# A Mamba block and a quantised FFN on one core: the second weight part on VectorE, batch 0's block-diagonals through DRAM, and a new order

## The reference

```python
# cross attention in name: a selective scan over ctx_1024, gated by layernorm(x)
x  = einsum('bld,ed->bel', ctx, in_proj_w)            # 4 x 256 x 256
u  = silu(causal_conv4(x) + conv_b)
x_dbl = einsum('bdl,ed->bel', u, x_proj_w)
dt_low, B, C = split(x_dbl, [8, 16, 16])
dt = softplus(einsum('brl,dr->bdl', dt_low, dt_proj_w) + dt_proj_b)
for l in range(256):                                   # per channel d, state n
    h = h * exp(dt[l] * A) + dt[l] * u[l] * B[l]
    y[l] = sum_n h * C[l]
y  = (y + D * u) * silu(z)                             # z = layernorm(x_in)
x  = x_in + tanh(g_xattn) * y.T
# FFN on layernorm(x), inputs quantised to 8 bits per row, 256 -> 2*704 -> 256
x13 = quant(layernorm(x)) @ w13.T ; x1, x3 = split(x13)
g   = rmsnorm(relu(x1)**2 * x3) * norm_w
out = x + tanh(g_ffn) * (quant(g) @ w2.T)
```

## Time and profile before

| what | value |
|---|---|
| time of three runs | 192.03, 193.95, 194.18 us, median 193.95 |
| the profiled execution | 194.1 us, its span 192.3, mean granted clock 0.982 |
| busy: PE, DVE, ACT, POOL | 175.6, 165.0, 153.3, 123.2 us |
| DMA | 22.47 MB in 27314 packets |
| chain that ended last | PE 64%, DVE 11%, issue 9%, DMA 5%, POOL 4%, ACT 4% |

### The profile page before, as it was taken

How to read it: one execution, slowest core, us unless ns; L and a number is a source line. 1 busy time by engine, 2 the same in 40 slices (tenths; PEclk the granted TensorE clock), 3 DMA queues, 4 the chain that set the end, 5 groups by cost and what they waited for, 6 DMA issues and landing times.

```text
span 192.3 us, 3413 instructions
## 1 busy us (share of the span) xinstructions
PE 175.6 (91%) x1106; PEld 139.3 (72%) x1106; DVE 165.0 (86%) x267; ACT 153.3 (80%) x388; POOL 123.2 (64%) x88
## 2 busy tenths in 40 slices
PE   3978889998699999999999999999996999998994
PEld 1745867876689978966798786868764576786783
DVE  0699995999967999999999997998999989996462
ACT  3468996999929999999999998987994979375630
POOL 3020575993869799749999586999980997440000
PEclk9999978999799999999999999999999999999999
DMA  4794960058970634696530038851007100001011
GB/s 83 235 294 142 367 213 0 1 26 206 406 266 20 205 122 12 110 346 216 172 109 0 10 4 136 302 164 60 0 0 238 38 0 0 3 6 51 1 56 56
DMA packets 27314, 22.47 MB, mean 117 GB/s; under 512 B 15152, under 2 KB 21024, under 8 KB 27296
## 3 DMA queue, kind: packets, MB, share of 16 engines
q1 hardware_dynamic: 26752, 22.25, 40.3%
q10 hardware_dynamic: 544, 0.01, 0.2%
HBM read 18.98 MB, written 3.27 MB: 116 GB/s over the span
## 4 chain that ended last, share of the span: by engine, by line
PE 64%; DVE 11%; issue 9%; DMA 5%; POOL 4%; ACT 4%; SPq 3%; POOLq 0%; DVEq 0%
PE m_ps L1078 25%; PE y_ps L1102 12%; PE w_ps L1132 10%; PE w_ps L1149 4%; DMA ctx_in<-in_ctx 3%; POOL hb L409 3%; DMA cs<-c_rows 2%; PE w_ps L1043 2%; DVE hb L889 2%; PE y_ps L1090 1%; PE w_ps L1035 1%; DVE gt L956 1%; PE w_ps L1140 1%; DVE xc L814 1%; PE w_ps L1158 1%
## 5 line engine op out<-in xcount | busy, mean ns | idle before, releaser
L409 POOL TENSOR_TENSOR hb<-hb,cs 128x1024 f32<-128x1024 f32 x31 | 73.6, 2388 | 4.5 <-DVE hb L900 4.0
L900 DVE TENSOR_TENSOR_SCAN hb<-dA,m_ps 128x1024 f32<-128x1024 f32 x30 | 67.9, 2276 | 5.9 <-PE m_ps L1078 3.8
L1078 PE MATMUL m_ps<-bd,duT 128*128 128x256 f32 (+1 forms) x216 | 59.7, 420 | 1.5 <-ACT duT L703 0.8
L688 ACT ACTIVATE dA<-dt,nega 128x255 f32<-128x255 f32 (+1 forms) x144 | 54.9, 465 | 0.0
L1078 PEld LDWEIGHTS m_ps<-bd,duT 128*128 128x128 f32 x216 | 40.8, 199 | 12.0 <-issue 5.2
L1102 PE MATMUL y_ps<-identf,hb 128*128 128x128 f32 x256 | 33.2, 278 | 0.3 <-POOL hb L409 0.2
L1102 PEld LDWEIGHTS y_ps<-identf,hb 128*128 128x128 f32 x256 | 29.5, 143 | 4.4 <-issue 1.7
L1132 PE MATMUL w_ps<-w13T,xqT 128*128 128x352 bf16 x192 | 30.3, 313 | 0.1
L1132 PEld LDWEIGHTS w_ps<-w13T,xqT 128*128 128x128 bf16 x192 | 18.6, 98 | 9.6 <-ACT xqT L725 0.5
L1149 PE MATMUL w_ps<-w2T,iqT 128*128 128x256 bf16 x144 | 16.5, 273 | 0.0
L424 POOL TENSOR_TENSOR gw<-gg,normw 128x704 f32<-128x704 f32 x7 | 12.8, 1829 | 5.3 <-DVE gg L942 5.3
(11 more groups left out here) (143 smaller groups left out, 273.7 us busy)
## 6 DMA issues: line engine op xcount, KB each, us to landing
cs<-c_rows SPq DMA_DIRECT2D x16, 512.0 KB, 5.8
bd<-b_diag SPq DMA_DIRECT2D x10, 512.0 KB, 7.0
b_diag<-zeros SPq DMA_DIRECT2D x1, 2048.0 KB, 9.9
gw<-in_L_ffn_w SPq DMA_DIRECT2D x1, 1408.0 KB, 9.2
x<-in_x SPq DMA_DIRECT2D x1, 1024.0 KB, 5.4
out<-ctx_in SPq DMA_DIRECT2D x8, 128.0 KB, 1.7
ru<-in_L_ffn_w SPq DMA_DIRECT2D x1, 704.0 KB, 8.9
bd<-b_rows SPq DMA_DIRECT2D x2, 256.0 KB, 3.6
```

The lines of the kernel that those rows point to most:

```text
L409: E.tensor_tensor(h_g, h_g, cs[:, s0:s0 + sn, l0:l0 + ln], ALU.mult).then_inc(hc_end if (b, i, h) == OUT_END else hc_ok[h], 1)
L688: last = act_fn(dA_g[:, s, 1:ln], dt[:, p, h, l0 + 1:l0 + ln], ACT.Exp, scale=nega[:, h, s0 + s:s0 + s + 1])
L900: V.tensor_tensor_scan(hb[:, k % 3, h], dA[:, k % 2, h].rearrange("p n l -> p (n l)"), m_ps[:, h], 0.0, ALU.mult, ALU.add).then_inc(scan_o ...
L1078: last = T.matmul(m_q[:, :, c * P - l0:(c + 1) * P - l0], duT[:, p, c, h * P:(h + 1) * P], bd[:, (s0 + sn // 2 * q) // GN, c, n0:n0 + sn / ...
```

## The change

Two steps change engine or way, and all five lists of `PLAN` are written anew.

1. `w_mid` (nine copies of float32 to bfloat16) runs on VectorE.
2. Batch 0 gets its block-diagonals through the DRAM scratch like the others: `bT` on TensorE and `bd` on VectorE are gone; `bput/0.0` and `bget/0.0` to `bget/0.3` come to the sync queue, and `zero` and the first loads change places. For batch 0 `bget` waits for `bput` alone.

```diff
 def diagonals(b, g):
-    return sum(1 for a in range(1, b + 1) if a == BATCH - 1 or not by_pool(a, g))
+    return sum(1 for a in range(b + 1) if a == BATCH - 1 or not by_pool(a, g))
...
-        dt/0.1 bd/0.1 scan0/0.0 scan1/0.0 w_res/0.3 lowc/1.0 scan0/0.1 scan1/0.1 conv/2.0 scan0/0.2 series/1.0
+        dt/0.1 w_res/0.3 w_mid/0.1 lowc/1.0 w_mid/0.2 scan0/0.0 w_mid/0.3 scan1/0.0 scan0/0.1 scan1/0.1 conv/2.0
...
+        bget/2.0 bget/2.1 bget/2.2 bget/2.3 bput/3.0 cget/2.1 bget/3.0 mput/3.0 bget/3.1 cput/3.0 cget/2.2 cget/2.3
...
                 elif name == "bput":
                     sp.wait_ge(free["dve"], emptied("xdbl", b, 0))
-                    if b == 1:
+                    if b == 0:
                         sp.wait_ge(d_zero, 16)
...
                 elif name == "bget":
-                    sp.wait_ge(b_put, 16 * HALVES * b)
-                    taken(b, i)
+                    sp.wait_ge(b_put, 16 * HALVES * (b + 1))
+                    if b:
+                        taken(b, i)
...
-                elif name == "w_mid":
-                    n_, parts = wp_cols(i)
-                    act.wait_ge(free["dve"], emptied("w", 0, i))
-                    act_fn(parts[1], wres[:, i % 3, 0:n_], ACT.Copy).then_inc(wmid_ok, 1)
...
+                elif name == "w_mid":
+                    n_, parts = wp_cols(i)
+                    dve.wait_ge(free["dve"], emptied("w", 0, i))
+                    V.tensor_copy(parts[1], wres[:, i % 3, 0:n_]).then_inc(wmid_ok, 1)
...
-                        if b == 3:
-                            dve.wait_ge(b_put, 16 * HALVES)
+                        dve.wait_ge(b_put, 16 * HALVES * (b - 1))
...
-                            if b:
-                                g = (s0 + sn // 2 * q) // GN
-                                pe.wait_ge(b_got[g], 16 * diagonals(b, g))
-                            elif c < HALVES - 1:
-                                pe.wait_ge(bd_ok, i // 2 + 1)
-                            else:
-                                pe.wait_ge(free["dve"], emptied("bT", b, i // 2))
+                            g = (s0 + sn // 2 * q) // GN
+                            pe.wait_ge(b_got[g], 16 * diagonals(b, g))
```

More of the change, by code:

```diff
@@ L101 @@
+        down/2.1 iqT/3.1 down/3.0 down/3.1
     """,
     "act": """
[L103 to L106 removed]
@@ L132 @@
-        final/1.1 gate/3.2 gate/3.3 gated/3.1 absmax/3.1 scale2/3.1 quant2/3.1 final/2.0 final/2.1 outscale/3.1
-        final/3.0 final/3.1
+        winT/0.0 conv/0.0 conv/0.1 clamp/0.0 xstat/0.0 clamp/0.1 u/0.0 xstat/1.0 xstat/2.0 u/0.1 xstat/3.0 dtwT/0.0
+        lowc/0.0 gates/0.0 conv/1.0 series/0.0 clamp/1.0 dt/0.0 series/0.1 w_res/0.0 w_mid/0.0 w_res/0.1 w_res/0.2
+        dt/0.1 w_res/0.3 w_mid/0.1 lowc/1.0 w_mid/0.2 scan0/0.0 w_mid/0.3 scan1/0.0 scan0/0.1 scan1/0.1 conv/2.0
+        series/1.0 cubic/1.0 dt/1.0 scan0/0.2 w_res/0.4 w_res/0.5 du/1.0 scan1/0.2 clamp/2.0 scan0/0.3 w_mid/0.4
@@ new lines @@
+        scan1/0.3 w_mid/0.5 scan0/1.0 w_res/0.6 scan1/1.0 yz/0.0 w_res/0.7 x1/0.0 w_mid/0.6 scan0/1.1 absx1/0.0
+        w_mid/0.7 w_res/0.8 lowc/2.0 scan1/1.1 w_mid/0.8 scan0/1.2 conv/3.0 quant1/0.0 series/2.0 cubic/2.0 dt/2.0
+        scan1/1.2 gate/0.0 gate/0.1 du/2.0 scan0/1.3 scan1/1.3 gate/0.2 gate/0.3 clamp/3.0 absmax/0.0 scan0/2.0
+        yz/1.0 absmax/0.1 x1/1.0 scale2/0.0 lowc/3.0 scan1/2.0 scan0/2.1 absx1/1.0 outscale/0.0 quant1/1.0
+        series/3.0 scan1/2.1 quant2/0.0 scan0/2.2 gate/1.0 dt/3.0 gate/1.1 scan1/2.2 scan0/2.3 gate/1.2 gate/1.3
```

112 lines of the change are left out of this document (44 added, 68 removed).

## The result

| | kernel before | changed kernel |
|---|---|---|
| executions beside each other | 192.03, 192.13, 193.95, 194.18 us | 196.92, 197.99, 198.88, 200.64 us |
| median | 193.04 us | 198.44 us |
| profiled execution, its span, granted clock | 194.1, 192.3 us, 0.982 | 200.64, 198.7 us, 0.965 |

The ratio is **1.027, interval 1.022 to 1.032**: slower, where 1.006 was forecast; 198.44 us still lies in the range. Some executions of every kernel here take over 1.5% longer than its fastest, most of them at a lower granted clock, and every ratio with an interval is of the others alone, while the medians beside it are of all executions.

What follows compares the result with a forecast made beforehand. TensorE and VectorE were taken as both nearly full from 59.02 to 133.25 us. +5.1 us up to yz/2.0 and -3.9 in the tail gave +1.2 on the profiled 194.1, forecast 195.1 us, range 187.8 to 198.7.

Steps and rivals of the forecast that it cites:

- Part 1: Up to the first scan: block-diagonals fetched through the sync queue make it start at 34.7 us, +4.4 on 30.29.
- w13 to 21: Sync queue before the first mix: the w13 load, ahead of the element writes, is done at 21 us.
- The 5.5 us behind w13: Sync queue: batch 0's element writes let bget/0.0 go out 5.5 us after w13, at 26.5.
- Part 2: First scan of batch 0 to that of batch 1: w2 stall goes, VectorE is late next; 29.1 us, before 30.55.
- the 1.8 us of holds: First scan of batch 0 to that of batch 1: VectorE instructions held beside GpSimd products, 3 x 0.6 us.
- Part 3: To the last sum of batch 2: VectorE, later than TensorE, counts; yz/2.0 starts at 138.4, +5.1 us in all.
- less four waits of together 1.9 us that more lateness eats: VectorE, scan0/1.0 to yz/2.0: four waits (0.97, 0.42, 0.21, 0.28 us) vanish because VectorE is later, 1.9 us subtracted.
- Part 4: Tail from yz/2.0: C rows for out0/3.1 come 4.6 us sooner, the up-projection gains 3.4; taken as -3.9 us.
- what is late next is the up-projection of batch 2: Tail: its start hangs on quant1/2.0, which moves up by about as much as the C rows; estimated gain 3.4 us.
- A: Rival, faster: element writes not queued behind w13, copies not held; first scan at 31.8, total 188.8 us; chance 0.32.
- B: Rival, slower: five copies and du/1.0 each held 1.2 us or more by GpSimd products; +3.6, 198.7 us; chance 0.12.
- C: Rival, slower: cget/2.1 behind bput/3.0 brings out0/2.1's C rows late, 2.3 us charged; 197.4 us; chance 0.12.

Runs made afterwards that it cites:

- e13: The changed kernel itself, measured again one set later; median 198.33 us against 193.55 for the kernel before.
- e14: Kernel before with only final/0.0 moved right behind x1/2.0 and final/0.1 behind the first of the two scans; median 198.82 us against 193.55.
- e7: Kernel before with cget/3.3, bget/3.2 and bget/3.3 issued ahead of the first two stores on the sync queue; 198.29 us, ratio 1.030.
- the probes: 16 two-element VectorE copies added to the kernel before, ahead of the scans of batches 1 and 2; 15.1 us in all reading SBUF, 2.3 reading PSUM.
- e1: Changed kernel with cget/2.1, cget/2.2 and cget/2.3 ahead of bput/3.0 on the sync queue again; 203.04 us, ratio 1.049.
- e17: Kernel before, its order kept, with w_mid copies on VectorE and batch 0's block-diagonals through DRAM; 196.87 us, ratio 1.021.
- e3: Kernel before with only the nine w_mid copies moved from ScalarE to VectorE; 197.28 us, ratio 1.011.
- e5: Kernel before with only batch 0's block-diagonals sent through the DRAM scratch; 194.62 us, ratio 1.008.
- e9: Kernel before with 16 added two-element VectorE copies from SBUF ahead of the scans of batches 1 and 2; median 207.58 us.
- e10: Kernel before with 16 added two-element VectorE copies reading PSUM ahead of the scans of batches 1 and 2; 197.7 us, ratio 1.037.
- e18: Kernel before with l_w2 issued early and 12 more idle transposes on TensorE, run in five rounds; 189.75 us, ratio 0.982.
- e11: Kernel before with l_w2 moved four places up on the sync queue, ahead of bput/1.0; 191.5 us against 190.8, ratio 0.998.

## Why the prediction was wrong

The terms of the sum, against e13 (clock 0.983, +4.4 us on the profiled run of before; forecast +1.2):

| part | forecast | measured | |
|---|---|---|---|
| 1, first scan | +4.4 | +2.2 | the load ahead was done earlier |
| 2, to scan0/1.0 | -1.4 | -1.1 | right |
| 3, to yz/2.0 | +2.1 | +4.9 | mis-sized |
| 4, tail | -3.9 | -1.6 | mis-sized: what was next was VectorE |

**Part 1: too dear by 2.2 us.** The term that was mis-sized is "w13 to 21": it landed at 18.3 (18.6 in e13), and bget/0.0 went out at 24.03 (23.75), between the two ends. The 5.5 us behind w13 came as 5.7 and 5.2, but they are not a fixed term: in the seven traces where batch 0's element writes stand behind w13, bget/0.0 goes out 7.9 to 8.8 us after the first of them is issued (8.4 in both of these), and 4.5 to 5.9 behind the landing of w13. (The late end of the forecast is 21 + 7.4 + 4.4 = 32.8, not 32.5; nothing hangs on it.) The clock was low, as said: from 24.3 us for 13.7 in the first execution, from 25.2 for 6.8 in e13.

**Part 2: right**, with other contents, and so in part by luck. The w2 stall went and VectorE became the bound; the copies here took 0.34 to 0.40 us; the 1.8 us of holds came as 2.7, on the softplus steps and `du/1.0`, not on copies.

**Part 3: the step that failed** is "less four waits of together 1.9 us that more lateness eats". VectorE's idle time in the stretch did not shrink by 1.9 us, it grew by 1.5, from 2.8 to 4.3: this one term is wrong by 3.4, more than the 2.8 by which the sum is. Its waits of 0.15 us and more are 3.3 us after (1.9 before): 0.90 for GpSimd's `cubic/3.0` (0.97 before), 0.54 at a gate, 0.53 and 0.39 at yz/1.0 and yz/2.0, 0.69 ahead of a scan, 0.25 at absmax/1.1. So what VectorE waits for came later too; why each did was not followed up. The other terms: copies 1.5 (1.3 forecast), absmax 0.8 (0.9), holds 1.1 net (1.8), namely 2.1 on L848, less 1.0 that the kernel before had elsewhere.

**Part 4: the step that failed** is "what is late next is the up-projection of batch 2 ... it moves up by about as much". out0/3.1 came 12.5 us behind yz/2.0 (11.1 forecast, 15.7 before), so the C rows were earlier as said. But quant1/2.0 came 10.5 us behind yz/2.0 instead of 12.3, so it moved up by 1.8 and not by 3.4 or more. What was next was VectorE. Windows from yz/2.0 to yz/3.1, before and in e13:

```profile
133.25:170.12 36.87, 34.61 (x232) 24.74 (x231) 34.88 (x62) 28.36 (x86) 25.68 (x17) 1.00 0.12 36
139.28:173.92 34.64, 32.84 (x223) 24.07 (x222) 32.98 (x61) 25.47 (x77) 25.73 (x16) 1.00 0.13 39
```

Before, VectorE was idle in only 2.0 of 36.9 us there, after in 1.7 of 34.6. yz/3.0 comes 4.7 us sooner behind yz/2.0 (19.0 us), but yz/3.1 only 2.2, and 1.9 of these are time in which VectorE is no longer busy there: absmax/1.1 (0.8) and 1.1 us of holds (1.6 instead of 2.7). The last stretch gives 0.6 back. Where the same wait is taken away alone, in e14 and e7, the holds grow instead and it costs.

**The rivals.** A (bget/0.0 before 25 us) had its condition met and was still wrong: its first scan at 31.8 is near the 32.5 to 32.8 measured, but it has no holds (27.3 us for part 2, 29.5 measured) and takes the eaten waits and the tail from the forecast. B was wrong in its place: copies of 0.50 us. Its mechanism is the one that the probes show, on other instructions. C had its condition met (lowc/3.0 at 107.06, in e13 at 104.37, and a wait of 5.3 to 5.6 us), and its time of 197.4 is near; but the near time is no proof, since C leaves out the 3.4 us of part 3 and what part 1 and 4 had wrong. e1 takes its wait away and gets slower, so nothing is regained by that; as e1 has 2.4 to 3.0 us more of holds and a stretch of low clock in its place, the price of the wait itself stays open.

**What caused the 2.7%**: shown is that the two engine changes, put alone into the old order, cost 2.1% together (e17), and each costs something by itself (e3 1.1%, e5 0.8%). How the 2.1% splits between them is not settled: at equal clock it is 1.9% for e3 and 0.4% for e5. Whether the new order adds to it (0 to 1%) stays open.

## What to carry to other kernels

A wait of GpSimd beside a nearly full VectorE may be worth having: before valuing its removal, list VectorE's short instructions with SBUF operands alone (reductions left out) that would then meet a running product, at up to one product (2.3 us) each. Subtract a wait as "eaten" by lateness only when what it waits for doesn't move too. And in a hand-made order the price of a part is better read by doing it alone in the old order than by undoing it in the new one, and from the whole time of several executions.

## What was not expected of the hardware

- A two-element copy from SBUF takes up to 2.26 us beside a GpSimd product of 2.36, from PSUM 0.13 to 0.16 (e9, e10).
- The exclusion goes both ways: in e3 a product that started at 73.53 took 2.86 us instead of 2.36, with a copy of 0.41 us at 73.75.
- Filling TensorE's short waits (0.7 and 1.3 us) and removing one of 2.6 us kept the granted clock at 1.0 in five of six executions, where the kernel before beside them had 0.974 to 0.991 in all eleven (e18). Removing the long wait alone gave nothing (e11), but the filling alone was not run, so which of the two is needed stays open.
